# A four-layer kernel: in its F layers each batch runs attention and then its experts, with the second batch's preparation inside the first's experts

## The reference

```python
h = _rms(x, n1_w)                               # x: layer-normed input
q = _rms(heads(wq), qn_w); k = _rms(heads(wk), kn_w); v = heads(wv)   # 16 heads of 8
scores = jnp.einsum('bhqd,bhkd->bhqk', q, k) * HD ** (-0.5)
attn = jax.nn.softmax(jnp.where(causal, scores, -jnp.inf), axis=-1)
x = x + (attn @ v @ wo.T, first 32 columns zero)
xf = _rms(x, n2_w)
wts = the two largest of softmax(xf @ gate_w.T), normed, for 4 experts
o0 = _gelu(xf @ e0_up.T) @ e0_down.T
o1 = _silu(xf @ e1_w1.T) * (xf @ e1_w2.T) @ e1_down.T
o2 = _gelu(_gelu(_gelu(xf @ e2_l1.T) @ e2_l2.T) @ e2_l3.T) @ e2_l4.T
o3 = _gelu(_gelu(xf @ e3_down.T) @ e3_up.T) @ e3_out.T
return x + (wts[0] * o0 + wts[1] * o1 + wts[2] * o2 + wts[3] * o3, first 32 columns zero)
```

## Time and profile before

| | us |
|---|---|
| three runs | 1207.23, 1208.35 (median), 1209.22 |
| the profiled execution | 1207.07 |
| its span, first to last instruction | 1205.2 |
| busy: PE / DVE / ACT / POOL | 674.5 / 867.5 / 506.5 / 403.4 |
| first F layer, first small step to last add | 467.82 to 784.23 |
| second F layer | 886.08 to 1199.65 |
| mean granted TensorE clock | 0.759 of full speed |

### The profile page before, as it was taken

How to read it: one execution, slowest core, us unless ns; L and a number is a source line. 1 busy time by engine, 2 the same in 40 slices (tenths; PEclk the granted TensorE clock), 3 DMA queues, 4 the chain that set the end, 5 groups by cost and what they waited for, 6 DMA issues and landing times.

```text
span 1205.2 us, 11485 instructions
## 1 busy us (share of the span) xinstructions
PE 674.5 (56%) x4014; PEld 333.1 (28%) x4014; DVE 867.5 (72%) x1306; ACT 506.5 (42%) x752; POOL 403.4 (33%) x334
## 2 busy tenths in 40 slices
PE   4990000040004004479899799963264799978997
PEld 2450000040004003222222556631243122225655
DVE  6899999999999995856657733269959557667212
ACT  3423000122220001579999322243034899973321
POOL 1250847600006602226765000006802566650000
PEclk9985555555555556779999799987565899997999
DMA  2250006172000020223310000000003242100001
GB/s 92 70 140 1 1 0 140 35 168 63 13 14 14 0 35 0 84 75 116 97 33 22 1 1 1 1 0 1 0 0 115 63 142 54 54 1 1 1 1 35
DMA packets 30258, 50.71 MB, mean 42 GB/s; under 512 B 4472, under 2 KB 14328, under 8 KB 29176
## 3 DMA queue, kind: packets, MB, share of 16 engines
q1 hardware_dynamic: 29432, 49.32, 15.2%
q10 hardware_dynamic: 768, 0.66, 0.3%
HBM read 20.98 MB, written 16.92 MB: 31 GB/s over the span
## 4 chain that ended last, share of the span: by engine, by line
DVE 47%; PE 23%; ACT 16%; issue 10%; POOL 1%; DMA 1%; ACTq 1%; POOLq 0%; SPq 0%; DVEq 0%
ACT PX L1445 10%; PE PS L1330 6%; PE PS L1308 5%; PE PS L1350 4%; PE PS L1289 3%; DVE D L813 2%; DVE S L817 2%; DVE P L814 2%; DVE PS L871 2%; DVE PRD L870 2%; DVE mag L1031 2%; DVE PA L772 2%; ACT P L688 2%; DVE RO L837 2%; DVE RP L832 2%
## 5 line engine op out<-in xcount | busy, mean ns | idle before, releaser
L1445 ACT ACTIVATE PX<-PS 128x1024 f32<-128x1024 f32 (+1 forms) x320 | 268.1, 1016 | 12.1 <-PE PS L1271 12.1
L1224 POOL TENSOR_TENSOR PX<-PX,maskf 128x256 f32<-128x256 f32 (+1 forms) x192 | 173.4, 931 | 125.0 <-ACT PX L1445 124.5
L1289 PE MATMUL PS<-PX,VA 128*32 128x512 f32 (+3 forms) x1536 | 166.2, 503 | 22.3 <-POOL PX L1224 14.5
L1617 DVE SCALAR_TENSOR_TENSOR X<-PS,wts,X 128x96 f32<-128x96 f32 x128 | 38.4, 315 | 118.2 <-PE PS L1350 103.9
L1271 PE MATMUL PS<-QS,KS 64*128 64x512 bf16 (+3 forms) x768 | 107.8, 339 | 16.7 <-issue 11.4
L1554 DVE RECIPROCAL DEN<-DEN 128x512 f32<-128x512 f32 x32 | 107.3, 3353 | 1.1
L580 PE MATMUL PS<-ones,HT 64*128 64x1 f32 x64 | 13.0, 348 | 152.0 <-ACT HT L672 152.0
L947 POOL TENSOR_TENSOR PRQ<-PA,LQK 128x2048 f32<-128x2048 f32 (+15 forms) x16 | 39.9, 2520 | 151.8 <-DMA WS<-S 138.6
L1552 DVE LOAD_MASK_SELECT DEN<-PS x32 | 0.4, 14 | 107.2 <-PE PS L1289 93.5
L591 PE MATMUL PS<-awout,V 64*128 64x128 f32 x64 | 13.3, 422 | 110.5 <-DVE vss L820 110.5
L1308 PE MATMUL PS<-HT,fw 128*128 128x512 f32 x144 | 71.2, 638 | 3.9 <-DVE HG L1584 2.6
(11 more groups left out here) (264 smaller groups left out, 1649.5 us busy)
## 6 DMA issues: line engine op xcount, KB each, us to landing
QS<-qs_d SPq DMA_DIRECT2D x32, 196.0 KB
qs_d<-QP SPq DMA_DIRECT2D x24, 256.0 KB, 3.9
ks_d<-QP SPq DMA_DIRECT2D x24, 256.0 KB, 4.0
KS<-ks_d SPq DMA_DIRECT2D x32, 192.0 KB
K<-LQK SPq DMA_DIRECT2D x16, 256.0 KB
W<-WS SPq DMA_DIRECT2D x16, 256.0 KB, 4.1
qkv_d<-CY SPq DMA_DIRECT2D x3, 1024.0 KB, 3.9
LQK<-qkv_d SPq DMA_DIRECT2D x8, 256.0 KB, 4.9
```

Of the source, the lines that this page charges most:

```text
L1224: pool.tensor_tensor(block, block, bcast(maskf[:], 1, 2 * halves), ALU.mult).then_inc(probs_masked, 1)
L1289: last = pe.matmul(PS[32 * h:32 * h + 32, SCORES_BANKS + qc, c0:CH], VA[b][:, kt, h, :], px[:, i % 2, at:at + CH - c0], start=(kt == 0), s ...
L1445: act.activation(tile(PX[u % PDEPTH][:]), tile(PS[:, k:k + 2, :]), ACT.Exp).then_inc(probs_ready, 1)
```

## The change

- The F layer runs batch by batch: preparation of batch 0, attention of batch 0 (80 units), its experts, attention of batch 1, its experts. Of batch 1's preparation the projection and the squares come ahead of the first attention, its norming stands in VectorE's order after the first join of the attention; turning, rounding and splitting stand between the pieces of batch 0's experts.
- The experts go chunk by chunk: all four experts of one chunk, then of the next. The router works on a batch (8 tiles) and stands after the first chunk's last gelu on ScalarE. The last downs of the first chunk are made behind ups of the second.
- The joins: for each group of heads VectorE adds numerator and denominator of 512 queries to AO and to a wider DEN (two passes), and divides once for each 512 queries, after the last group (`divided`). The projection and the second norm work on 512 queries.
- All thirds are on GpSimd. For batch 1 it makes them after the first attention's masks.
- Expert tiles share memory with PX and with batch 0's part of QKV (in the order below PX0 is what HA was, PX1 HB, PX2 HC, PX3 HF, PX4 and QKV HS, PX5 HG). The output is stored in two halves, the first one after batch 0 of the last layer.

The core of the diff:

```diff
+                if u == HALF:
+                    thirds(1)
...
-            for c in range(NCH):
-                if c:
-                    pe.wait_ge(up_read, hidden + c)
-                    up(c, 0, F_E1A)
-                    pe.wait_ge(h1_ready, gated + c)
-                    up(c, 2, F_E1B)
-                    down1(c - 1)
...
+            for b in range(B):
...
+                for u in range(b * HALF, (b + 1) * HALF + LAG):
+                    if u < (b + 1) * HALF:
+                        scores(u)
+                    if u - LAG >= b * HALF and u - LAG in TILE_END:
+                        sums(u - LAG)
+                    if u == b * HALF + 78:
+                        out_project(c0, O_BANKS)
+                if b == 0:
+                    pe.wait_ge(qk_normed, rep * B + 2)
+                    qk_turned(CB, SIDE_BANKS)
+                turned(c0, B + c0, O_BANKS)
+                pe.wait_ge(ht_read, 2 * rep * NCH + NCH + c0 + 1)
+                up(c0, 0, F_E1A)
+                up(c0, 2, F_E1B)
...
+                up(c0, 0, F_E2)
...
+                out_project(c1, SIDE_BANKS)
+                pe.wait_ge(h1_ready, gated + 1)
+                up(c0, 2, F_E0)
...
+                down1(b, 0)
+                pe.wait_ge(up_read, read + 2)
+                up(c0, 0, F_E3, 1)
+                turned(c1, B + c1, SIDE_BANKS + 1)
+                pe.wait_ge(up_read, read + 3)
+                mid(2, 0, [HA[:, k, :] for k in range(2)])
+                router(b)
...
+                if b == 0:
+                    pe.wait_ge(router_read, rep * B + 1)
+                    qk_turned(CB + 1, SIDE_BANKS)
+                pe.wait_ge(up_read, read + 6)
+                up(c1, 0, F_E1A)
+                pe.wait_ge(up_read, read + 7)
+                up(c1, 2, F_E1B)
+                if b == 0:
+                    pe.wait_ge(rest_ready, 2 * (rep + 1) * NCH)
+                    shifts_turned(1, SIDE_BANKS)
+                pe.wait_ge(up_read, read + 8)
+                up(c1, 0, F_E2)
+                pe.wait_ge(h1_ready, gated + 2)
+                up(c1, 2, F_E0)
+                down(b, 0)
...
             def heads_out(it, qc):
...
+                    v.scalar_tensor_tensor(out=AO[:, t:t + CH], in0=o, scalar=mine, in1=AO[:, t:t + CH],
+                                           op0=ALU.mult, op1=ALU.add)
+                    v.scalar_tensor_tensor(out=DEN[:, t:t + CH], in0=o, scalar=after, in1=DEN[:, t:t + CH],
+                                           op0=ALU.mult, op1=ALU.add).then_inc(o_read, 1)
...
+            def divided(c):
+                t = c * CH
+                v.wait_ge(o_read, OBANKS + (rep * B + c // CB) * 2 * NG + 2 * (NG - 1) + c % CB + 1)
+                link(v.stream_shuffle(DINV[:], DEN[:, t:t + CH], [(r + HD) % 32 for r in range(32)]))
+                link(v.reciprocal(DINV[:], DINV[:]))
+                v.tensor_tensor(AO[:, t:t + CH], AO[:, t:t + CH], DINV[:], ALU.mult).then_inc(ao_ready, 1)
...
+                divided(c1)
+                gate(b, 0)
+                second_squares(c1, SIDE_BANKS)
+                second_normed(c1)
+                logits(b)
+                weights(b)
+                v.wait_ge(x_sum, rep * NCH + c1 + 1)
+                add1(b, 0)
+                if b == 0:
+                    q_k_rest(CB + 1, SIDE_BANKS)
+                gate(b, 1)
+                add_rest(b, 0)
...
+                gelu(b, 0, 7, 2, 2, HC)
+                router(b)
+                if b == 0:
+                    high(CB + 1, SIDE_BANKS)
+                silu(b, 1)
+                if b == 0:
+                    mid(CB + 1)
+                    shifts(1, SIDE_BANKS)
+                gelu(b, 1, 2, 0, 2, HA)
```

More of the change, by code:

```diff
@@ L242, in hybrid_kernel @@
[L242 to L256, removed]
+                HG1 = sb("HG1", [P, 2, CH], at=sF)
@@ new lines, in project @@
+            def project(b, bank_of, free):
+                for i in range(TB):
+                    t = b * TB + i
+                    if i % TPC == 0:
+                        pe.wait_ge(ht_read, 2 * rep * NCH + b * CB + i // TPC + 1)
+                    if free[i]:
+                        pe.wait_ge(qkv_read, rep * TILES + free[i])
+                    pe.matmul(PS[:, bank_of[i], 0:3 * D], HT[:, t * P:(t + 1) * P], fw[:, 0:3 * D], start=True,
+                              stop=True).then_inc(qkv_full, 1)
@@ L1250, in f_tensor, with qk_turned, shifts_turned @@
+            def qk_turned(c, bank):
+                for n in range(2):
+                    for i in range(TPC):
+                        last = pe.transpose(PS[:, bank + n, i * P:(i + 1) * P], QKS[:, c * TPC + i, n * D:(n + 1) * D],
+                                            ident[:])
+                    last.then_inc(t_full, 1)
+            def shifts_turned(b, bank):
                 pe.wait_ge(shifts_ready, rep * B + b + 1)
-                for c in chunks:
-                    k = banks.take()
+                for j in range(CB):
+                    c = b * CB + j
@@ L1421, in f_scalar, with router @@
+            def router(b):
+                tb = slice(b * TB, (b + 1) * TB)
+                ask.wait()
+                act.activation(pr[:, tb], lg[:, tb], ACT.Exp).then_inc(to_dve, 1)
+            act_sqrt(act, ask, stat[:])
+            act_sqrt(act, ask, stat[:])
+            for c in range(CB):
+                turned(c, c)
+            project(0, (2, 3, 4, 5, 6, 7, 0, 1))
+            act_sqrt(act, ask, qst[:, 0:TB])
             q_squares(0)
-            high(0)
+            high(0, 2)
@@ L1446, in f_scalar @@
[L1446 to L1455 removed]
+            high(1, 4)
@@ new lines, in f_scalar, with exps @@
+            mid(0)
+            shifts(0, 6)
+            mid(1)
+            for c in range(CB, NCH):
+                turned(c, c - CB)
+            project(1, (2, 3, 4, 5, 0, 1, 6, 7))
+            act_sqrt(act, ask, qst[:, TB:2 * TB])
+            def exps(b):
+                for u in range(b * HALF, (b + 1) * HALF):
+                    heads, c0 = ATT[u][3:]
+                    halves = len(heads) // 2
+                    tile = lambda t: t.rearrange("p k (n q) -> p k n q", n=halves)[:, :, :, 0:CH - c0]
+                    k = 2 * (u % DEPTH)
+                    act.wait_ge(scores_ready, rep * NA + u + 1)
+                    act.wait_ge(probs_used, rep * NA + u + 1)
+                    act.activation(tile(PX[u % PDEPTH][:]), tile(PS[:, k:k + 2, :]), ACT.Exp).then_inc(probs_ready, 1)
```

703 lines of the change are left out of this document (374 added, 329 removed).

## The result

The changed kernel takes 1250.18 us (median of 4 runs, 1245.99 to 1253.24), the kernel before 1208.78 beside it (4 runs): a ratio of 1.034, 95% interval 1.030 to 1.038. The forecast was 1246.0 with a range of 1228 to 1258. The profiled execution took 1247.59 us, its span is 1245.8, 40.6 more than before. Two of the four runs took 1246.0 and 1247.6, the other two 1252.8 and 1253.2; the trace is of one of the shorter, so what the longer two spent some 5 us on is not shown.

A forecast was written before the change was run, and what follows sets the result against it. TensorE was taken to bound the experts, ScalarE attention. Terms -5.9 + 1.4 + 0.5 + 24.2 gave +20.2 us a layer, +40.4 for two, less 1.5 at the final store: 1207.07 to 1246.0 us, range 1228 to 1258.

The forecast's parts named there:

- Start of a layer: Preparation before the first exp: less of batch 1's work ahead of batch 0's, first exp 5.9 us earlier a layer.
- Attention: Exps in two halves: +1.4 us a layer for filling the pipeline twice, +0.5 for norming beside masks.
- The term of the shared interfaces: In attention, batch 1's norming on VectorE delays GpSimd's masks and so scores: +0.5 us a layer, bounds 0 to 3.
- that rival, at 1233.9: In attention, the joins set the pace, so 12.1 us of ScalarE's waits for scores go: 1233.9 us, chance 0.07.
- Experts: From last exps through join and experts, both batches: 146.35 us against 122.1 before, +24.2 us a layer.
- Gap (a): In each batch's experts, TensorE waits for the router weights' chain: 7.25 us in batch 0, 6.75 in batch 1.
- The turn (b): In the experts, the second chunk's turn waits for a root behind a table load: 1.1 us a batch.
- the last gelu (c): At the experts' end, the last downs wait for a batch's last gelu: 1.3 us, now twice a layer.
- The clock (e): TensorE at its lower clock after idling: +1.8 us behind each 5 to 7 us gap, 1.0 at each join.
- That TensorE never waits: Rival in the experts: waits find cover, no clock is lost, 21.8 us a layer fall away: 1202.4 us, chance 0.07.
- The second batch's stack: Before the second attention: forecast hidden with 13 us of cover; as a rival, 4 us late, 1254 us, chance 0.04.
- pause beyond the table load: Rival on ScalarE: each table switch also drains, 1.38 us by the skill, an estimated 1257 us, chance 0.02.

The follow-up runs named there:

- experiment 3: From the changed kernel, VectorE's norming of the second batch's q and k runs right after its squares, beside the stores: 1246.88 us, ratio 1.0316 to the kernel before.
- experiment 1: From the changed kernel, ScalarE's router exp of each half moved ahead of the last two gelus: 1214.29 us, ratio 1.0045 to the kernel before.
- experiment 4: From the changed kernel, earlier router exp and norming beside the stores together: 1211.96 us; with three scores also ahead of the first batch's last downs: 1205.47 us.
- experiment 5: From the kernel before, only the joins changed to two passes each and one division per chunk at a batch's end: 1208.58 us, ratio 1.0004.
- experiment 2: From the changed kernel, the 24 ranking steps of the router weights left out in each half: 1228.32 us, ratio 1.0164 to the kernel before.
- experiment 7: From the kernel before with the first batch's rests taken early, only two pieces turned before the first batch's projection: 1207.45 us, ratio 0.9998 to the kernel before.
- experiment 6: From the kernel before, first batch's rests ahead of the second's squares, second's root behind the first's conversions: 1202.41 us, again 1203.67 us.

## Why the prediction was right

*The whole.* Forecast +20.2 a layer and -1.5 at the end; the trace shows +20.9, +20.0 and -1.85 (3.70 us from the last add to the end against 5.55). The layers ahead of and between the F layers gave +1.5, from no edit. 1246.0 against 1247.59 in the profiled execution. The mechanism was right, TensorE waiting for the weights' chain; that the total came so close is in part luck. The start was forecast 1.5 and 1.0 us too dear, attention 1.8 and 1.0 too cheap, and these cancel; within the experts gaps that were put too high and clock that was put too low cancel in the same way.

*Start of a layer.* Right in kind, too small: -5.9 forecast, -7.4 and -6.9 found. Before, the reduce began 17.4 us after the layer's start, now 15.5: 1.9 (forecast 2.4). From there to the first third it was 18.4 us and is 14.6: 3.8 (forecast 3.5). That is the forecast's 5.9, within 0.2. The rest came from GpSimd's thirds. I took them at 3.1 us each, but that was the mean of two unlike ones. Before, the first took 2.12 us and the second, beside VectorE's slow passes, 4.17. With no norming beside them they take 2.13 and 2.12 in this layer, 2.22 over all eight. The second third before, and the group now (mean in ns behind the busy time):

```profile
505.73 4.17 POOL L1185 TENSOR_TENSOR QP<-QR,QP 128x1024 bf16<-128x1024 f32 x1
...
L1206 POOL TENSOR_TENSOR QP<-QR,QP 128x1024 bf16<-128x1024 f32 x8 | 17.8, 2221 | 146.6 <-ACT QP L1487 146.5
```

The trace of before had shown the slow passes of VectorE there, and I did not ask what they did to the GpSimd instruction beside them.

*Attention.* +1.4 and +0.5 forecast, +3.7 and +2.9 found. Without the norming beside the masks (experiment 3) the two halves take 137.8 us in the first F layer, as before the change, and 138.8 in the second, 1.5 more: the split costs nothing to 1.5 us, and my 1.4 was at its upper end. The term of the shared interfaces was mis-sized: 0.5 for a price of 3.3 and 1.3 (1.2 and 1.2 between experiments 1 and 4), once just above my upper bound of 3. The joins were free (experiment 5), and that rival, at 1233.9, is out.

*Experts.* +24.2 forecast, +24.7 and +24.0 found, and the places were right. The first up came 7.5 and 6.8 us after the last exp (7.95 and 7.2). Gap (a) was 6.82 us in batch 0 (7.25), and 4.08 + 1.56 = 5.64 in batch 1 (6.75): the steps took 6.2 us, not 6.6. The turn (b) waits 0.93 (1.1), the last gelu (c) 1.11 (1.3). Nearly all of these were put a little too high. The clock (e) was put too low: behind the gaps the slow ups cost 2.15 and 1.9 us, the turn and the downs beside them another 0.8 and 0.9 (1.8 in all forecast for each), and the first three ups of a batch took 7.11 and 6.94 us for 5.2 at the full clock, three times 1.72 (1.0 forecast for each join). Experiment 1 removes gap and clock together, experiment 2 in proportion to the chain; so 16.5 of the 24 us have this one cause.

*The rivals.* That TensorE never waits got 0.07 and did not happen, but it was one line away: with the exp moved it came to 1214, and with two more edits to 1205. Of my price for it, 21.8 us a layer, 17.6 stood for the gaps (a) and the clock behind them; the moved line gives 16.5. The waits for the root and the clock at the joins stay. The second batch's stack was ready in time: no transfer was under way from 654.3 to the first score at 666.30, 12 us later, close to the 13 of cover that were forecast. The clock times given with that cover (708.2, 725.0, 738, and 742 in the rival) are some 74 us too late: they count from the old last exp at 662.15, not from 588. As all are shifted alike, the cover is not touched. No pause beyond the table load showed: gelu, load and exp stand back to back at 623.08, 624.12 and 625.41, the exp 0.01 us behind the load's end. The 1.38 us that the Trainium skill (ScalarE: Activation LUTs, What ACT_TABLE_LOAD costs) adds to each switch are not seen here.

## What to carry to other kernels

A step that is a chain of small instructions on one engine costs nothing only as long as the bounding engine has work that doesn't depend on it; when stages are cut in two, count that cover for each half, and look where in each queue the chain's first instruction stands: to start it 6.9 us earlier gave some 16.4 us a layer here, to leave out 24 of its 34 steps some 10.4. Overlap pays by the idle time of the engine that bounds: here TensorE was 97% busy in the experts and ScalarE 97% in attention, so running one batch's preparation inside the other's experts had only the start of a layer to win. When an idle stretch is filled, work out what the filler itself waits for; of 6.2 us won at the join 1.5 were left.

## What the runs showed of the hardware

VectorE's passes over two operands in SBUF and GpSimd's passes lengthen each other both ways: VectorE's 1.22 us became 1.68 to 3.03, GpSimd's third up to 4.17 instead of 2.12, nine of its masks 10.03 instead of 7.40.

The granted clock at the start of a layer does not follow from the instruction order alone. The same sixteen matmuls, behind the same 16 us of idle and the same turns, took 6.06 us in the trace of one kernel (granted clock 0.89) and 7.65 in that of another (0.70) whose order is the same up to there. Whether it differs between kernels or between executions is not shown. A gain of 1 or 2 us worked out across such a stretch can vanish, as in experiments 3 and 7.

The first F layer started at 467.65 to 470.83 us in the thirteen traces, with no edit ahead of it, and at 470.52 and 468.44 in two executions of the same kernel (experiment 6), so times of a stage are compared from its own start.
